# Cross-attention and gated mixture kernel: a written-out opening, six drafts, and GpSimd issuing the first stores of U

## What is computed

```
xn  = layernorm(x)
q, k, v = xn @ Wq, ctx @ Wk, ctx @ Wv           # 8 heads of 64
x   = x + softmax(q k^T / 8) v @ Wo + bo        # cross-attention
h   = layernorm(x)
rw  = gating(h, sim_matrix, gates)              # 16 experts: cosine logits, relu, top-2 fallback, softmax
q, k, v = sum_e rw_e * (h @ proj_e)             # one head of 64, per expert projections
a   = softmax(causal(q k^T / 8)) v
out = x + sum_e (a * rw_e) @ o_proj_e
```

## Time and profile before

| | |
|---|---|
| median of 3 runs | 2558.81 us (2558.7 to 2559.17) |
| the profiled execution, its own time | 2557.84 us |
| its span | 2556.0 us |
| TensorE busy | 2476.8 us |
| VectorE busy | 2124.5 us |
| ScalarE busy | 1584.6 us |
| GpSimd busy | 1102.1 us |
| mean granted TensorE clock | 0.986 |

### The profile page before, as it was taken

How to read it: one execution, slowest core, us unless ns; L and a number is a source line. 1 busy time by engine, 2 the same in 40 slices (tenths; PEclk the granted TensorE clock), 3 DMA queues, 4 the chain that set the end, 5 groups by cost and what they waited for, 6 DMA issues and landing times.

```text
span 2556.0 us, 54410 instructions
## 1 busy us (share of the span) xinstructions
PE 2476.8 (97%) x17308; PEld 2426.4 (95%) x17308; DVE 2124.5 (83%) x6126; ACT 1584.6 (62%) x5126; POOL 1102.1 (43%) x1741
## 2 busy tenths in 40 slices
PE   5699999999999999999999999999999999999997
PEld 4699999999999999999999999999999999999997
DVE  5688888888888888888888888888888888888885
ACT  5566666666666666666666666666666666666642
POOL 2144444444444444444444444444444444444442
PEclk8799999999999999999999999999999999999998
DMA  5655555565555555565565556465565556465531
GB/s 170 212 180 172 185 172 178 157 191 175 180 179 177 178 172 186 151 199 173 173 190 172 171 176 188 148 207 171 165 199 172 164 176 196 143 207 169 165 118 46
DMA packets 288070, 441.48 MB, mean 173 GB/s; under 512 B 20356, under 2 KB 199492, under 8 KB 279723
## 3 DMA queue, kind: packets, MB, share of 16 engines
q1 hardware_dynamic: 218155, 369.84, 44.4%
q10 hardware_dynamic: 69632, 68.17, 10.9%
HBM read 254.86 MB, written 181.83 MB: 171 GB/s over the span
## 4 chain that ended last, share of the span: by engine, by line
PE 81%; DVE 6%; POOL 5%; issue 3%; ACT 3%; DMA 1%; SPq 0%; POOLq 0%; DVEq 0%; ACTq 0%
PE bank_b L554 12%; PE bank_b L555 12%; PE bank_b L556 12%; PE bank_c L554 5%; PE bank_c L555 5%; PE bank_c L556 5%; PE bank_a L555 4%; PE bank_a L554 4%; PE bank_a L556 4%; PE bank_a L699 3%; PE bank_a L663 2%; PE bank_a L675 2%; PE bank_a L664 2%; DVE both L1346 1%; PE bank_a L638 1%
## 5 line engine op out<-in xcount | busy, mean ns | idle before, releaser
L1454 DVE SCALAR_TENSOR_TENSOR acc<-bank_b,rw,acc 128x192 f32<-128x192 f32 x1792 | 654.6, 410 | 109.0 <-PE bank_b L556 106.7
L554 PE MATMUL bank_b<-wqkv_hi,x2T_lo 128*128 128x384 f32 (+1 forms) x2048 | 720.4, 352 | 2.9 <-ACT acc L1076 1.9
L555 PE MATMUL bank_b<-wqkv_lo,x2T_hi 128*128 128x384 f32 (+1 forms) x2048 | 693.8, 339 | 0.0
L556 PE MATMUL bank_b<-wqkv_hi,x2T_hi 128*128 128x384 f32 (+1 forms) x2048 | 690.3, 337 | 0.0
L1798 POOL TENSOR_TENSOR mixs_lo<-mix,mixs_hi 128x512 fp32r<-128x512 f32 x254 | 378.2, 1520 | 165.1 <-ACT mixs_hi L1152 165.1
L1046 ACT ACTIVATE probs<-bank_a,s_max 128x77 f32<-128x77 f32 x1024 | 317.8, 330 | 207.1 <-DVE s_max L1384 207.1
L554 PEld LDWEIGHTS bank_b<-wqkv_hi,x2T_lo 128*128 128x128 f32 x2048 | 386.7, 189 | 5.2 <-ACT acc L1076 2.4
L555 PEld LDWEIGHTS bank_b<-wqkv_lo,x2T_hi 128*128 128x128 f32 x2048 | 387.0, 189 | 0.0
L556 PEld LDWEIGHTS bank_b<-wqkv_hi,x2T_hi 128*128 128x128 f32 x2048 | 385.1, 188 | 0.0
L1152 ACT ACTIVATE mixs_hi<-mix 128x512 fp32r<-128x512 f32 x256 | 159.9, 633 | 208.7 <-DVE mix L1495 208.7
L554 PE MATMUL bank_c<-wo_hi,mixs_lo 128*128 128x256 f32 x1000 | 280.9, 281 | 3.7 <-POOL mixs_lo L1798 3.7
(11 more groups left out here) (253 smaller groups left out, 6389.4 us busy)
## 6 DMA issues: line engine op xcount, KB each, us to landing
gq<-g_dram SPq DMA_DIRECT2D x63, 1232.0 KB, 5.6
rw_all<-rw_dram ACTq DMA_DIRECT2D x128, 512.0 KB, 6.9
uo<-u_dram SPq DMA_DIRECT2D x63, 1024.0 KB
g_dram<-draft SPq DMA_DIRECT2D x105, 462.0 KB
u_dram<-draft SPq DMA_DIRECT2D x127, 308.0 KB
g_dram<-mixs_lo SPq DMA_DIRECT2D x63, 462.0 KB
xt<-in_x_dram SPq DMA_DIRECT2D x64, 256.0 KB, 4.7
out_dram<-mix SPq DMA_DIRECT2D x62, 256.0 KB, 3.9
```

Of the source, the lines that this page charges most:

```text
L554: nc.tensor.matmul(dst, lhs[1], rhs[0], start=start, stop=False)
L555: nc.tensor.matmul(dst, lhs[0], rhs[1], start=False, stop=False)
L556: return nc.tensor.matmul(dst, lhs[0], rhs[0], start=False, stop=stop)
L1454: V.scalar_tensor_tensor(acc[:, t, k, :], src, rw[:, t, e:e + 1], acc[:, t, k, :], ALU.mult, ALU.add).then_inc(b_evac, 1)
```

## The change

The steps -1 and 0 no longer run through the loop's `step`; each engine has its own written-out list for them. What it does:

- Steps -1 and 0 on TensorE: k0 and k1 of group 1, then at once `a_y` and `b_xT` of batch 0 (into a bank of stage c, `bank_y`), then g0, g1, `b_qkv(0, 0)` and `(0, 1)`, and the other jobs with `b_qkv(0, 2)` to `(0, 5)` among them. ScalarE, VectorE and GpSimd follow this order; the weight splits 8 to 15 are spread over it.
- The opening: ScalarE evacuates the context before it splits Wk; v1 comes after s3; the splits of Wo come after g7 instead of before g6 (ScalarE), and between the scores (VectorE); the squares of `sim_matrix` come after g7 instead of between k2 and g2.
- Six drafts for group 1: g4 and g5 get drafts 4 and 5.
- SyncE: the loads of x for batch 1 and of G for batch 1, and the weights 7 and 8, stand elsewhere; the U stores of group 0 for batches 1 and 2 (12 DMAs) are taken from SyncE and issued by GpSimd (`store_u` there), SyncE keeps the 12 copies into `uo` (`first_u`). `load_u` waits for both; the first k and v copies of stage c wait for drafts 4 and 5.
- From step 1 on the order is unchanged on all engines.

```diff
-               ("g", 5), ("v", 0), ("g", 6), ("g", 7), ("s", 0), ("s", 1), ("v", 1), ("s", 2), ("s", 3), ("u", 0), ("u", 1),
+               ("g", 5), ("v", 0), ("g", 6), ("g", 7), ("s", 0), ("s", 1), ("s", 2), ("s", 3), ("v", 1), ("u", 0), ("u", 1),
...
     DRAFT = {"E1": 0, "E2": 2, "E3": 3, "M1": 1, "L1": 0, "L2": 1}
-    FIRST_USE = (0, 1, 4, 5)
+    FIRST_USE = (0, 1, 4, 5, 2, 3)
+
+    def draft_of(gm, kind, f):
+
+        return f if (gm, kind) == (1, "g") and f in (4, 5) else DRAFT.get(SLOT[kind, f])
...
+        def bank_y(n):
+            return bank_a("Y") if n else banks_c[0]
...
-        SPLIT_AFTER = {("k", 1): (W_V,), ("v", 0): (W_O - 1, W_O), ("s", 7): (W_QKV, W_QKV + 1)}
+        SPLIT_HI = {("k", 1): (W_V,), ("g", 7): (W_O - 1, W_O), ("s", 7): (W_QKV, W_QKV + 1)}
+        SPLIT_LO = {("k", 1): (W_V,), ("s", 1): (W_O - 1,), ("s", 2): (W_O,), ("s", 7): (W_QKV, W_QKV + 1)}
...
@@ SyncE @@
+            def first_u(f):
+                sp.wait_ge(u_evac, at(H, 0, f))
+                for e, row, chunk, p0, count in first_rows(f):
+                    sp.dma_start(uo[p0:p0 + count, chunk, :, :].rearrange("p l c -> p (l c)").bitcast(F32),
+                                 first_drafts[(H + f) % FIRST_DRAFTS][row:row + count, e * 2 * C:(e + 1) * 2 * C].bitcast(F32)
+                                 ).then_inc(uo_rows[f // 2], 16)
...
             load_x(1)
             load_g(1)
-            for f in range(H):
-                store_u(0, f)
-            for i in range(-1, B + 2):
+            load_weights((7, 8))
+            for f in range(0, H, 2):
+                first_u(f)
+            load_g(2)
+            load_weights((11,))
+            load_ctx(2)
+            load_u(1)
+            load_x(2)
+            turn(-1, "E2")
...
@@ TensorE @@
+            turn(-1, "E0")
+            turn(-1, "E1")
+            a_y(0, 0)
+            a_y(0, 1)
+            b_xT(0, 0)
+            b_xT(0, 1)
+            turn(-1, "E2")
+            turn(-1, "E3")
+            b_qkv(0, 0)
+            b_qkv(0, 1)
+            turn(-1, "M1")
+            turn(-1, "M2")
+            b_qkv(0, 2)
+            turn(-1, "L1")
...
+            for i in range(1, B + 2):
                 step(i)
...
@@ ScalarE @@
-            split_weights(W_K)
             for kind, f in OPENING:
                 if kind == "ct":
                     j_ct(f)
+                    if f == 0:
+                        split_weights(W_K)
...
@@ GpSimd @@
+            def store_u(f):
+                slot = (H + f) % FIRST_DRAFTS
+                pool.wait_ge(u_evac, at(H, 0, f))
+                for b, k0, k1, row in u_rows(f):
+                    if b:
+                        G.dma_start(u_dram[0, b, :, :].rearrange("(h k) x -> k h x", h=H)[k0:k1, f // 2 * 2:f // 2 * 2 + 2, :],
+                                    first_drafts[slot][row:row + k1 - k0, :].bitcast(F32).rearrange("p (h x) -> p h x", h=2)
+                                    ).then_inc(first_rest_out[slot], 16)
...
             a_p(0, 1)
+            store_u(0)
+            store_u(1)
             power(1, 0)
+            for f in range(2, H):
+                store_u(f)
             a_p(1, 0)
             a_p(1, 1)
 
-            for i in range(-1, B + 2):
+            power(0, 1)
+            a_xb(1)
...
```

More of the change, by code:

```diff
@@ L312, in xattn_moe_kernel @@
         pad_done = sem("pad_done")
+        first_rest_out = [sem(f"first_rest_out{k}") for k in range(FIRST_DRAFTS)]
+        uo_rows = [sem(f"uo_rows{k}") for k in range(HB)]
         acc_opened = sem("acc_opened")
@@ L1672, in _ @@
                     a_psum(1, f - 6)
-                for k in SPLIT_AFTER.get((kind, f), ()):
+                for k in SPLIT_LO.get((kind, f), ()):
                     split_weights(k)
-            for i in range(-1, B + 2):
+            turn(-1, "E0")
+            turn(-1, "E1")
+            a_y(0)
+            ln2_a(0)
+            b_xT(0, 0)
+            b_xT(0, 1)
+            for k in range(3):
+                b_norm(0, k)
+            turn(-1, "E2")
+            turn(-1, "E3")
+            b_z(0, 0)
+            b_z(0, 1)
+            b_top(0)
+            b_index(0)
+            split_weights(8)
+            turn(-1, "M1")
+            turn(-1, "M2")
+            b_wsum(0)
+            turn(-1, "L1")
+            b_qkv(0, 2)
+            turn(-1, "L2")
+            turn(0, "E0")
+            split_weights(9)
+            turn(0, "E1")
+            split_weights(10)
+            ln1_a(2)
+            turn(0, "E2")
+            for k in range(3):
+                a_pT(1, k)
+            b_qkv(0, 3)
+            split_weights(11)
+            turn(0, "E3")
+            turn(0, "M1")
+            split_weights(12)
+            a_xT(2)
+            b_qkv(0, 4)
+            turn(0, "M2")
+            split_weights(13)
+            b_qkv(0, 5)
+            a_y(1)
+            turn(0, "L1")
+            turn(0, "L2")
+            split_weights(14)
+            split_weights(15)
+            for i in range(1, B + 2):
                 step(i)
@@ L1802, in step @@
                 nxt, ahead, now, before, earlier = i + 2, i + 1, i, i - 1, i - 2
-                normed, rows, probs_of = [n if n >= start else -1 for n, start in ((nxt, 2), (ahead, 2), (ahead, 1))]
                 def do(n, fn, *k):
@@ L1811, in step @@
                 do(now, power, 1)
-                do(rows, a_p, 0)
-                do(rows, a_p, 1)
-                do(normed, power, 0)
+                do(ahead, a_p, 0)
+                do(ahead, a_p, 1)
+                do(nxt, power, 0)
                 do(before, b_sum, 0)
@@ L1829, in _ @@
             a_p(0, 1)
+            store_u(0)
+            store_u(1)
             power(1, 0)
+            for f in range(2, H):
+                store_u(f)
             a_p(1, 0)
             a_p(1, 1)
-            for i in range(-1, B + 2):
+            power(0, 1)
+            a_xb(1)
+            b_route_1(0)
+            b_route_2(0)
+            b_w(0)
+            b_rw(0)
+            power(2, 0)
+            a_xb(2)
+            for i in range(1, B + 2):
                 step(i)
```

419 lines of the change are left out of this document (227 added, 192 removed).

## The result

The changed kernel takes 2554.34 us (median of 20 runs, 2550.39 to 2556.35), against 2559.56 us for the kernel before (20 runs beside it): a ratio of 0.998, 95% interval 0.9973 to 0.9986. It is faster, but by 5.2 us and not by 14.3, and lies above the range.

A forecast was written before the change was run, and what follows sets the result against it. Steps from step 1 on were taken as bound by TensorE's work, so the gain is how much earlier step 1 begins: 5.3 + 0.5 + 9.3 - 0.8 = 14.3 us, median 2544.5 us, range 2538 to 2552.5.

The forecast's parts named there:

- Start to s0: From the kernel's start to the scores s0 of the opening: 5.3 us earlier, in three parts.
- (c): Opening: splits of Wo moved behind g6 and g7, whose evacuation s0 waits for: 3.5 us.
- (a): Opening: ScalarE evacuates the context before splitting Wk, so k0 starts at 12.35, 0.3 us earlier.
- s0 to k0 of group 1: Opening from s0 on, Wo splits between the scores: 0.5 us more gained, 5.8 in all, k0 at 65.7.
- k0 of group 1 to step 1: Stretch ahead of step 1: 43.9 us instead of 53.2, 9.3 earlier, as draft, layernorm and routing waits go or shrink.
- The draft wait: ScalarE's wait for draft 1's store ahead of step 1 goes, since g4 and g5 get own drafts: 5.1 us.
- The layernorm's stand: Between `a_y(0)` and `b_xT(0)`, TensorE waits through the layernorm chain: 4.5 us in which all engines stand.
- Behind `b_xT(0)`: From 79.4 on VectorE has the longest list, 24.4 us plus 4.4 of waits; step 1 begins at 109.6.
- Behind step 1: After step 1 begins: 0.8 us given back, as weights 14 and 15 are split at the very end.
- The rivals that rested on this queue: GpSimd's DMAs cost 2.91 us each, 2552.3 us (chance 0.06); or GpSimd holds the second layernorm, slower, 2567.8 (0.03).
- The weights as the wait: Rival: ScalarE waits three times 2 to 2.5 us for late weights ahead of step 1; gain 7, 2551.8 us; chance 0.17.
- it does not do what it says: Rival: step 1 is held until loads of batch 2 and weights 14, 15 come; under 5 us remain, 2555; chance 0.04.

The follow-up runs named there:

- the second trace: The changed kernel run again with nothing edited, profiled a second time: 2554.09 us, ratio 0.998 (the traced execution 2552.01 us).
- the copies first: The change with U stores back on SyncE, those of u2 to u7 behind the last copy into `uo`: 2547.04 us, ratio 0.9956.
- copies first with four drafts: The copies first, but g4 and g5 of group 1 in drafts 0 and 1 again: 2553.67 us, ratio 0.9975.
- G ahead of both: The change with g0 and g1 ahead of `a_y(0)`, and g2, k2 and g3 ahead of `b_xT(0)`: 2551.47 us, ratio 0.9972.
- GpSimd's stores late: The change with GpSimd issuing the stores of u2 to u7 only once all copies into `uo` have landed: 2550.02 us, ratio 0.9969.
- The fillers: Identity transposes added: 14 ahead of `a_y(0)`, 17 ahead of `b_xT(0)` on the change, 2552.76 us; 17 ahead of `b_xT(0)` on the copies first, 2547.36 us.

## Why the prediction was wrong, step by step

**Start to s0: right within the spread.** Forecast 35.3; the two traces of the change show 36.43 and 35.10. (c), the splits of Wo, at 3.5 us, lies within the 2.3 to 3.6 us that putting them back cost. (a) did not come: k0 starts at 13.05 and 12.57, not at 12.35. ScalarE's table load is held by the context as forecast, from 7.44, but VectorE then waits 0.4 us for the high part of Wk and needs 2.2 us for its own part, not 1.7.

**s0 to k0 of group 1: wrong by 1.1 us.** I expected 0.5 us more; both traces give 0.6 back (s0 4.14 and 5.47 earlier, k0 3.54 and 4.88). I had only a sketch of this chain.

**k0 of group 1 to step 1: the step that failed.** 9.3 us forecast, 2.4 measured (53.2 to 50.8), 3.4 in the second trace. The forecast's 43.9 us were 3.5 until `a_y(0)` starts, 4.6 for `a_y(0)`, 4.6 until `b_xT(0)` and 31.2 behind that; measured were 6.9, 6.1, 4.8 and 33.0. Half of the miss is the first of these, which held no term for the landing of the copies. Compared with the copies first, where the same stretch takes 45.2 us (68.00 to 113.20), the missing part is 3.8 us until `a_y(0)` starts and 2.4 us in its own duration (6.1 against 3.7), less 0.6 us for what follows. I had priced neither the landing nor a slower `a_y(0)` behind it (the second trace has it at 5.3 us, so of the 2.4 us 1.6 are there in both). I wrote of SyncE's issues "This costs me nothing in the sum", because all that they gate is late anyway. That was true of the loads. It was not true of the copies into `uo`, on which `a_y(0)` waits: before the change they had until 82.69, and the change moves their consumer to 71, with the stores of the same pieces going out among them. I counted GpSimd's DMAs as an engine's time and SyncE's as a queue's, and did not ask what both put on the same DMA engines. The forecast of a landing was missing from the chain altogether. Of the rest of this step, with the copies in time, 8.0 of the 9.3 us are there.

**The draft wait, 5.1 us inside that step: right in size, wrong in being additive.** Alone in the old steps the earlier opening only lengthened it to 6.3 us; with late copies its removal was worth 0.7 at most; with the copies first 4.5 to 4.9. It and the copies' landing cover each other: while the one wait stands, taking away the other is worth 0.7 us (drafts) or 1.4 (copies first with four drafts, 6.4 against 5.0).

**The layernorm's stand: 4.8 us measured, 4.5 forecast.** Putting work into it moved the wait to the routing. That `b_xT(0)` stands at once behind `a_y(0)` cost no more than the other orders that were timed, clear of noise.

**Behind `b_xT(0)`: 1.8 us too short.** I had 31.2 us from its start to step 1, measured were 33.0 in the change and 32.8 with the copies first.

**Behind step 1: 3.0 us given back in the profiled pair, 0.8 forecast.** 1.4 go in the first step, 0.3 over sixty steps, 1.2 in the last 50 us, where the pipeline runs empty; in the trace with the copies first the whole loss behind step 1 is 2.1. Where it goes in the last stretch was not tried.

**GpSimd: right.** 1 us per issue taken, 0.8 measured, hidden; the power starts 0.24 us after VectorE begins the last operation on its input. The rivals that rested on this queue (2.91 us each, or the layernorm held) are out. With the stores late, GpSimd does become the one that the power waits for, by under 0.5 us.
The Trainium skill (DMA: Bandwidth & Descriptors, anatomy of one DMA on the SWDGE path) gives a DMA from GpSimd 2.0 us fixed and the bytes at 436 GB/s, for 152 to 308 KB 2.3 to 2.7 us as an estimate by that page. Here the engine was held for 0.8 us, so not for the transfer, and the data landed 3.4 to 9.3 us after the start of the issue, longer than by that rule; the DMA engines were 0.73 busy.

**The weights as the wait: no.** ScalarE has no wait for a load in this stretch. The case "it does not do what it says" had the right time, 2555, and the wrong reason: step 1 was not held by the loads of batch 2 or the last weights.

## What to carry to other kernels

When a change moves a consumer forward, list everything that it waits for with the time by which each had landed before, not only the engines' own chains: a transfer that lands before anyone needs it has no row in the waits, and appears as the new wait. Here the last copies into `uo` were issued by 74.3 us before the change, with their reader at 82.69. When two transfers of the same buffers leave together and only one has a reader soon, issue that one alone and the other behind it; here this order was worth 5.5 to 6.0 us by the gains, about as much as the whole change as it stood (5.2 to 5.7). And parts that remove waits on parallel paths don't add: time each of them with the others in place.

## What the runs showed of the hardware

An issue is not a fixed price. The same three copies (those of u6) took SyncE 2.3 us with the copies first, where the DMA engines were 0.45 busy between 62 and 65 us, and 6.9 us in the change, where they were 0.76 busy between 63 and 70, though GpSimd had issued the stores among them.

Of TensorE: whether the stores stand among the copies does not decide the clock between 48 and 68 us. The traces with the stores among them have 0.57 to 0.83 there, those with the copies first on SyncE 0.57 to 0.85; the 0.66 and 0.83 of the two windows above are one pair of these. In `a_y(0)` there is a pattern. In all seven traces in which it came out of a stand (2.75 to 5.0 us) it began at the lower of the two levels and took 5.1 to 6.5 us. In the six with the copies first on SyncE it came without a stand, had the full clock and took 3.6 to 3.7 us. The two other kernels without a stand there (G ahead of both, GpSimd's stores late) still began at the lower level and took 4.7 and 4.9 us, so a missing stand alone does not give the full clock. The fillers closed no stand and test nothing here. What decides between the two levels in such a stretch stays open.
